# A gated recurrence on one core: the instructions of a step in another order on five engine queues

## The reference

```
r = sigmoid(i_r + h_r);  z = sigmoid(i_z + h_z);  n = tanh(i_n + r * h_n)
h = (1 - z) * n + z * h          # i_* = agg w_ih^T + b_ih,  h_* = h w_hh^T + b_hh
```

## Time and profile before

| | |
|---|---|
| median of 3 runs | 805.92 us (805.19 to 806.97) |
| profiled execution | 805.15 us, its span 803.4 us |
| TensorE busy | 691.0 us, 86% of the span |
| VectorE busy | 598.2 us, 74% |
| ScalarE busy | 521.7 us, 65% |
| GpSimd busy | 300.5 us, 37% |
| mean granted TensorE clock | 0.970 |

### The profile page before, as it was taken

How to read it: one execution, slowest core, us unless ns; L and a number is a source line. 1 busy time by engine, 2 the same in 40 slices (tenths; PEclk the granted TensorE clock), 3 DMA queues, 4 the chain that set the end, 5 groups by cost and what they waited for, 6 DMA issues and landing times.

```text
span 803.4 us, 12366 instructions
## 1 busy us (share of the span) xinstructions
PE 691.0 (86%) x4091; PEld 574.1 (71%) x4091; DVE 598.2 (74%) x1461; ACT 521.7 (65%) x1083; POOL 300.5 (37%) x423
## 2 busy tenths in 40 slices
PE   3888879999889998989989898989989998986665
PEld 2567667788777777868767777768767777776544
DVE  4677986788877886798887886797886896696233
ACT  4455757577667777657667777667766667666433
POOL 4212423553333443453143443463233234452320
PEclk9899989999999999999999999999999999999779
DMA  6600002100000020400000020110000000210001
GB/s 148 177 11 1 2 0 56 54 1 4 4 5 2 1 55 2 131 27 2 5 7 1 1 56 9 59 40 1 6 5 1 1 1 2 65 40 6 6 1 53
DMA packets 47623, 21.08 MB, mean 26 GB/s; under 512 B 9032, under 2 KB 47560, under 8 KB 47560
## 3 DMA queue, kind: packets, MB, share of 16 engines
q1 hardware_dynamic: 47560, 20.29, 9.3%
HBM read 15.27 MB, written 4.19 MB: 24 GB/s over the span
## 4 chain that ended last, share of the span: by engine, by line
PE 48%; ACT 22%; DVE 21%; issue 5%; POOL 2%; DMA 1%; DVEq 0%; SPq 0%; POOLq 0%; ACTq 0%
PE bank L404 7%; PE bank L406 7%; PE bank L405 7%; ACT bank L872 4%; PE bank L390 4%; ACT rh L862 4%; ACT g_hi L860 3%; DVE g_lo L1301 2%; ACT xn L685 2%; DVE bank L1310 2%; DVE hd L1295 2%; PE bank L593 2%; PE bank L540 2%; PE bank L528 2%; PE bank L580 2%
## 5 line engine op out<-in xcount | busy, mean ns | idle before, releaser
L915 POOL TENSOR_TENSOR h_lo<-h,h_hi 128x512 fp32r<-128x512 f32 x64 | 83.7, 1308 | 299.3 <-DVE h_hi L1290 299.3
L404 PE MATMUL bank<-h_hi,whh_hi 128*128 128x512 f32 x240 | 103.2, 430 | 4.6 <-DVE rh L1307 4.6
L404 PE MATMUL bank<-g_hi,wc_hi 128*128 128x512 f32 x240 | 103.1, 429 | 0.0
L405 PE MATMUL bank<-g_hi,wc_lo 128*128 128x512 f32 x240 | 95.8, 399 | 0.0
L406 PE MATMUL bank<-g_lo,wc_hi 128*128 128x512 f32 x240 | 95.7, 399 | 0.0
L405 PE MATMUL bank<-h_hi,whh_lo 128*128 128x512 f32 x240 | 95.2, 397 | 0.0
L406 PE MATMUL bank<-h_lo,whh_hi 128*128 128x512 f32 x240 | 95.2, 397 | 0.0
L399 PE MATMUL bank<-edge,hn 128*128 128x128 f32 x640 | 84.7, 275 | 0.8 <-ACT hn L855 0.8
L869 ACT ACTIVATE gz<-bank,brz 128x512 f32<-128x512 f32 x80 | 55.0, 688 | 45.1 <-PE bank L406 43.0
L399 PEld LDWEIGHTS bank<-edge,hn 128*128 128x128 f32 x640 | 80.8, 192 | 4.2 <-issue 1.0
L1307 DVE SCALAR_TENSOR_TENSOR rh<-bank,rh 128x512 f32<-128x512 f32 x80 | 54.9, 686 | 34.8 <-ACT bank L867 34.8
(11 more groups left out here) (167 smaller groups left out, 1630.0 us busy)
## 6 DMA issues: line engine op xcount, KB each, us to landing
x_in<-in_x SPq DMA_DIRECT2D x8, 512.0 KB, 5.5
adj_in<-in_adj SPq DMA_DIRECT2D x8, 512.0 KB, 4.8
x_res<-in_x SPq DMA_DIRECT2D x16, 256.0 KB, 2.8
out_x<-x_res SPq DMA_DIRECT2D x16, 256.0 KB, 2.3
xz<-x_res SPq DMA_DIRECT2D x16, 50.0 KB
w_sb<-in_L_gnn_W SPq DMA_DIRECT2D x1, 640.0 KB, 5.2
w_sb<-in_L_gnn_W SPq DMA_DIRECT2D x5, 128.0 KB, 5.1
rows<-in_adj SPq DMA_DIRECT2D x32, 0.6 KB
```

The source lines that it names most:

```text
L404: nc.tensor.matmul(dst[:], w_hi, m_hi, start=start, stop=False)
L405: nc.tensor.matmul(dst[:], w_lo, m_hi, start=False, stop=False)
L915: nc.gpsimd.tensor_tensor(h_lo[q][:], h[q][:], h_hi[q][:].bitcast(f32), ALU.subtract).then_inc(sem["h_lo_new"], 1)
```

## The change

Each queue gets another order within the step; no instruction is added or taken away but waits.

- TensorE: the state products H, R and Z stand together at the head of the step. Then come the wait for `g_lo`, `turn_h(n+1)`, the wait for the eviction of H only where the even slot uses bank H (`h_bank_taken`), the even slot, the message products R, Z and I, `aggregate(n+1)`, and the odd slot after it.
- ScalarE: `hn(n+1)` stands ahead of the even slot. The tanh of I follows the tanh of Z at once, then `g_hi(n+1)`, and only then the odd slot.
- VectorE: after L1310 come `hd(n)`, `g_lo(n+1)` and the new state of `n`, and only then the odd slot.
- GpSimd: `h_lo` of step `n` is issued between the even and the odd slot of step `n`; before it stood after the odd slot.

```diff
+            def h_bank_taken(slot):
+                return due(slot, 1, TURN_OUT) or due(slot, 1, TURN2) or second_conv(slot) or due(slot, 1, BACK)
@@ TensorE
                 state_product(R_BANK, 0, q)
-                pe.wait_ge(sem["hb_ready"], n + 1)
-                beside(2 * n)
-                if n + 1 < ALL:
-                    turn_h(n + 1)
-                pe.wait_ge(sem["g_lo_ready"], n + 1)
-                message_product(R_BANK, 0, layer).then_inc(sem["gates_r"], 1)
                 if n:
                     pe.wait_ge(sem["z_ready"], n)
                 state_product(Z_BANK, 1, q)
+                pe.wait_ge(sem["g_lo_ready"], n + 1)
+                if n + 1 < ALL:
+                    turn_h(n + 1)
+                if h_bank_taken(2 * n):
+                    pe.wait_ge(sem["hb_ready"], n + 1)
+                beside(2 * n)
+                message_product(R_BANK, 0, layer).then_inc(sem["gates_r"], 1)
                 message_product(Z_BANK, 1, layer).then_inc(sem["gates_z"], 1)
                 if n:
                     pe.wait_ge(sem["h_new"], n)
                 message_product(I_BANK, 2, layer, True).then_inc(sem["gates_n"], 1)
-                beside(2 * n + 1)
                 if n + 1 < ALL:
                     aggregate(n + 1)
+                beside(2 * n + 1)
@@ ScalarE
-            turned_h(0)
-            for n in range(ALL):
+            def aggregate_hi(n):
                 act.wait_ge(sem["g_made"], n + 1)
                 nc.scalar.activation(g_hi[:], TG[:], ACT.Copy).then_inc(sem["g_hi_ready"], 1)
+
+            turned_h(0)
+            aggregate_hi(0)
+            for n in range(ALL):
                 act.wait_ge(sem["gates_h"], n + 1)
                 nc.scalar.activation(rh[:], H_BANK[:], ACT.Identity, bias=bhh[:, 2:3]).then_inc(sem["hb_ready"], 1)
-                beside(2 * n)
                 if n + 1 < ALL:
                     turned_h(n + 1)
+                beside(2 * n)
...
-                beside(2 * n + 1)
                 act.wait_ge(sem["pre_ready"], n + 1)
                 nc.scalar.activation(I_BANK[:], I_BANK[:], ACT.Tanh, bias=bih[:, 2:3]).then_inc(sem["n_ready"], 1)
+                if n + 1 < ALL:
+                    aggregate_hi(n + 1)
+                beside(2 * n + 1)
@@ GpSimd
-                if n and n <= ALL and (n - 1) % STEPS < SPLITS:
-                    low_half(n - 1)
                 beside(2 * n)
+                if n < ALL and n % STEPS < SPLITS:
+                    low_half(n)
                 beside(2 * n + 1)
@@ VectorE
-            for n in range(ALL):
-                if n:
-                    difference(n - 1)
+            def aggregate_lo(n):
                 dve.wait_ge(sem["g_hi_ready"], n + 1)
                 nc.vector.tensor_tensor(g_lo[:], TG[:], g_hi[:].bitcast(f32), ALU.subtract).then_inc(sem["g_lo_ready"], 1)
-                if n:
-                    new_state(n - 1)
+
+            aggregate_lo(0)
+            for n in range(ALL):
                 beside(2 * n)
...
                 nc.vector.scalar_tensor_tensor(I_BANK[:], rh[:], 0.5, I_BANK[:], ALU.mult, ALU.add).then_inc(sem["pre_ready"], 1)
+                difference(n)
+                if n + 1 < ALL:
+                    aggregate_lo(n + 1)
+                new_state(n)
                 beside(2 * n + 1)
-            difference(ALL - 1)
-            new_state(ALL - 1)
```

## The result

The changed kernel takes 813.96 us (median of 4 runs, 812.31 to 815.86) against 805.91 beside it (805.19 to 806.97): ratio 1.0100, 95% interval 1.0075 to 1.0124. The prediction was 799 us and faster; the time lies inside its range (784 to 815) but outside the forecast's own 788 to 804, on the wrong side.

What follows compares the result with a forecast made beforehand. TensorE was busiest, but an empty step was bound by a chain across engines. Terms -3.5 - 19.5 + 18 - 1.2 - 1.5 + 1 = -6.7 gave 798.4, forecast 799 us (own range 788 to 804); full range 784 to 815.

Steps and rivals of the forecast that it cites:

- The empty step: Step without slot work: state product Z ahead of the wait shortens its chain from 6.40 to 5.70 us.
- the largest loss: Layer 3's norms: statistics behind the new state, `power` behind `h_lo`; four steps a round of 10.41 us, +18 in all.
- the wait that would show it: Layer 3's norm steps: L685 waiting for L901, as the longest wait of ScalarE.
- Round 1: Five quite empty steps gain -3.5 us; its other fifteen put at nothing, bounds -10 to +12.
- Rival 2: Layer 3's norm chain costs nothing, so the +18 goes: about 781 us, chance 0.12.
- Layer 1's stage: Steps with layer 1's products: 4.9 us gained from ScalarE's order, 1.6 from `h_lo`; -6.5 a round, -19.5 in rounds 2 to 4.
- the other two are 10 us steps anyway: Layer 1's norms: two of four steps lie outside the last recurrence layer and were taken as 10 us already.
- contention that I had called released: `h_lo` beside the odd slot frees VectorE's L1172 (1.47 to 0.69 us): 0.8 for two steps a round, 1.6.
- Layer 2's stage: Eight steps with layer 2's tiles: 8.4 us against a mean of 8.46, so it stays; -0.4 a round.
- up to 0.83: VectorE's odd slot after the new state: cost per step where VectorE sets the step, 1.43 less 0.60.
- The ends: Tail gets its first norm later: +1 us, bounds 0 and 3.4.
- rival 1: Half clock in the norm stage: one such step a round, +14, 813 us; chance 0.33 together with another rival.

Runs made afterwards that it cites:

- e1: The changed kernel with GpSimd's `h_lo` put back behind the odd slot: 807.99 us, ratio 0.9972 to the kernel before.
- e3: The changed kernel with GpSimd's `h_lo` back behind the odd slot and VectorE's odd-slot `mean_variance` ahead of `hd`: 781.0 us, ratio 0.9675.
- e4: e3 with VectorE's `read_support2` of the odd slots between `g_lo` and the new state: 768.57 us, ratio 0.954.
- e7: The changed kernel with 14 unused state products ahead of TensorE's waits in the stretch behind the last step: 806.56 us, ratio 0.9983.
- e12: The kernel before with 14 unused state products ahead of TensorE's waits in the stretch behind the last step: 803.37 us, ratio 0.9927.
- e8: e5 with 14 unused state products ahead of TensorE's waits in the stretch behind the last step: 758.93 us, ratio 0.9399.
- e5: e4 with VectorE's edge weights and first statistics of the odd slots ahead of `hd`: 767.43 us, ratio 0.953.
- e6: The changed kernel with the wait for H's eviction taken in every step: 816.44 us, ratio 1.0129.

## Why the prediction was wrong

**What it had right.** The empty step (5.72), the mechanism of the largest loss, its four steps (10.29 against 10.41), the norm's start (7.55 after L1318, in the sum 7.60) and the wait that would show it, which is ScalarE's longest in those steps though not in the whole kernel. Round 1 came out by luck: five empty steps gave 3.4, and the other fifteen, taken at nothing, run from -1.8 to +2.0 and cancel. e1 to e3 show both links of that chain; without them 33 us go, more than the +18 that I charged, because the norms of layer 1, in the first and the last stage, had the same chain (25 us go in layer 3's norm stage, 5 in layer 1's, 5 in the last, and the stretch behind gives 2 back). Rival 2 put the kernel without the chain at 781 us, and e3 measured 781.0; that is partly luck, since e3's layer 2 stage was longer than I had it and its norm stage shorter.

**Layer 1's stage, -4.6 instead of -6.5 a round.** The step that failed is that layer 1's norms were put at nothing here ("the other two are 10 us steps anyway"). Two of its four steps took 9.33, under the 10.0 that I had. The other two took 10.86 and 10.81. Their rows after:
```profile
368.15 1.29 POOL L918 TENSOR_TENSOR h_lo<-hx,h_hi 128x512 fp32r<-128x512 f32 x1
...
368.48 1.51 DVE L1171 SCALAR_TENSOR_TENSOR gated<-gate_th,diff 128x512 f32<-128x512 f32 x1
...
379.91 0.88 ACT L689 ACTIVATE xn<-x_res,shift,rstd 128x128 f32<-128x128 f32 x2 [1.12 <-POOL shift L910]
...
388.13 0.66 DVE L1181 SCALAR_TENSOR_TENSOR mix<-mix,ex 128x512 f32<-128x512 f32 x1
```
The later step (10.81) is layer 1's norm in the chain; e3 takes it to 9.59, the earlier one to 10.40 and the stage to -6.4, the predicted gain. The earlier step also holds contention that I had called released: in the third step L1181 takes 0.66 as forecast, against 1.47 for L1172 in the earlier trace rows, but in the first L1171 now takes 1.51 beside GpSimd's `h_lo` of the first layer, and in the step behind this stage L1181 still takes 1.47. Over the whole kernel VectorE's three operations there (48 instructions) go from 42.8 us to 37.5: 7.8 released in two of them, 2.5 taken back in L1171. I had counted 4.8 in rounds 2 to 4, so this term was nearly right.
The Trainium skill, "SBUF — State Buffer", section "SBUF: two separate sides", has a lock of the shared port for a whole instruction. The trace agrees with it (1.51 beside 1.29), and the warning taken from it, that the block may only move to another pair, came true in part: for the 2.5 us of L1171, for 2.9 in `l3_finish` (L1234, three of 16 take 1.59 to 1.70 instead of 0.66) and for L1064 below.

**Layer 2's stage, +1.5 instead of -0.4 a round.** The failed step is "8.4 us, against 67.70 / 8 = 8.46 now. So the layer 2 stage stays where it is". The price was right: the second and third of these steps took 8.32 and 8.33. The comparison was wrong, for 8.46 is a mean over steps of 7.44 to 10.42. The second, below the new floor, grew to it (7.44 to 8.32), while only one above it shrank as much (10.42 to 9.31). e4 takes away the wait I had priced: that second step goes to 7.34, and the stage then gains 1.2 to 2.6 a round.
The last two steps grew too (7.81 to 8.64, 7.52 to 9.03), but mostly not by that wait: in e4 they still take 8.41 and 9.03. The last is VectorE's. It idles there only 0.73 us, ahead of `hd`, and its odd slot's L1064 now lies beside GpSimd's `h_lo`; the same work before, and then after:
```profile
466.67 1.22 DVE L1055 SCALAR_TENSOR_TENSOR blocks<-rowsI,dinv,gmask 100x100 f32<-100x100 f32 x5
```
```profile
465.76 1.29 POOL L924 TENSOR_TENSOR h_lo<-h,h_hi 128x512 fp32r<-128x512 f32 x1 [7.36 <-DVE h_hi L1299]
...
466.20 1.89 DVE L1064 SCALAR_TENSOR_TENSOR blocks<-rowsI,dinv,gmask 100x100 f32<-100x100 f32 x5
```
So this step pays the "up to 0.83" that the prediction named for VectorE's odd slot and kept out of its sum (0.82 here), and 0.67 of contention beyond that bound: 1.5 of the stage's 1.7 us in round 3. With e4's edit they stay.

**The ends, +5.4 instead of +1.** The clock, which the +1 had left out, and the order share the 4.1 behind the last step about equally in these executions (e7, e12). The 1.3 ahead of the first step is a stretch at the half clock in the setup that other kernels with the same setup have or lack from one execution to the next.

**The norm stage, +19.9 instead of +18.** This much of rival 1 came true: two of the twelve steps were at the lower clock for a part. One of them in the changed kernel (490.81 to 502.04), then the same step in e7, whose instructions up to there are the same:
```profile
490.81:502.04 11.23, 9.04 (x46) 7.63 (x46) 6.91 (x17) 7.67 (x18) 2.78 (x5) 0.85 0.01 1
```
```profile
489.34:499.63 10.29, 8.10 (x51) 6.71 (x51) 6.82 (x18) 7.73 (x18) 2.78 (x5) 1.00 0.01 2
```
The price is 0.94 in a step, not the 4.6 of a step wholly at the half clock, and it comes in some executions only. Four such steps (two more, of 1.3, in the layer 2 stage) make e7's profiled execution 4.4 us shorter than the changed kernel's before the products of no use begin; that is what one profile of this kernel leaves uncertain.

**Not settled**: what makes up the 2 us of order behind the last step. e8, which is e7 without the norm chain and with VectorE's other pieces early, needs 87.7 us there against 89.1, so these may be most of it; one profile of each is too little to say.

## What to carry to other kernels

In a step that several in-order queues share, one engine's order is worth something only with the others' (TensorE's part alone cost 2.4%, GpSimd's 5.4%): for each piece moved, ask which queue its answer stands in and behind what. Price each moved wait against every step's own length, not against the stage's mean, since the short steps pay and the long ones don't give it back; and where an engine has little idle time in a step, a piece that filled the rest of it is paid in full when it moves. Where the chain that ends last leaves TensorE waiting, look at the granted clock of that stretch before its work; matmuls of no use in the waits took 3 to 9 us out of 90 here.

## What the runs showed of the hardware that was not expected

- Matmuls that nobody reads, put into TensorE's waits, made four kernels faster: ratios to before of 0.9983 against 1.0100, 0.9399 against 0.953, 0.9197 against 0.9307, and 0.9927 against 1.
  The Trainium skill, "TensorE: Matmul & The Clock Gate", section "Why this matters for your kernels", advises against idle gaps between bursts of matmuls; the trace agrees, with 41 us at the half clock against 15 filled.
- An execution whose steps end 4.7 us earlier (e5 against e4) ended at the same time, for the stretch behind them took 5 us more, with 10 us more at the half clock. The same stretch of program had 41 us at the half clock in one execution and 48 in another (the changed kernel and e6), so a single profile doesn't tell whether an order has caused such a difference.
